# A two-layer transformer kernel: the first norm moved one step ahead, new engine orders in stage one, the rope sum in two pieces

## The reference

```python
xn = layernorm(x)
q, k, v = split(xn @ Wqkv.T + bqkv)            # then rmsnorm of q and k, rope, relu
vk = einsum('bhlp,bhld->bhpd', [v, 1], k)      # linear attention, 16 heads of 8
attn = einsum(vk, q)[..., :-1] / (einsum(vk, q)[..., -1:] + eps)
x = x + rmsnorm(attn @ Wout.T + bout) + quantise6(xn) @ quantise6(W).T + bias
```

## Time and profile before

| | |
|---|---|
| median of 3 runs | 407.57 us (407.36 to 408.72) |
| the profiled execution | 408.92 us, its span 407.1 us |
| busy: PE / DVE / ACT / POOL | 323.2 / 344.1 / 188.4 / 235.4 us |
| last operation of steps 1, 2, 6, 8, 9 | 29.79, 47.08, 109.98, 140.99, 154.96 us |
| routing begins on VectorE | 170.81 us |

### The profile page before, as it was taken

One profiled execution on the slowest core, in us unless ns is written; L12 is line 12 of the kernel. 1 busy time (PEld: TensorE's weight loads), 2 busy tenths in 40 slices (PEclk: granted clock), 3 DMA queues, 4 the chain that ended last, 5 costly groups with the idle time before them and its releaser, 6 DMA issues.

```text
span 407.1 us, 5016 instructions
## 1 busy us (share of the span) xinstructions
PE 323.2 (79%) x1455; PEld 237.0 (58%) x1455; DVE 344.1 (85%) x831; ACT 188.4 (46%) x501; POOL 235.4 (58%) x149
## 2 busy tenths in 40 slices
PE   0267696898898875805129999999999999999995
PEld 0136475777787765704016666666666666666662
DVE  3774997987887964599999899999999999999791
ACT  0535556778678656702122262624426262442521
POOL 9151573553644721095065959778695986867450
PEclk9986998999999999775758999999999999999999
DMA  7620000100100102220000000000000000000000
GB/s 184 209 77 1 2 0 1 54 37 17 52 22 32 53 27 96 91 52 0 1 0 1 2 0 27 2 26 0 0 28 1 26 2 26 1 2 26 0 26 27
DMA packets 13247, 12.49 MB, mean 31 GB/s; under 512 B 1548, under 2 KB 9924, under 8 KB 13220
## 3 DMA queue, kind: packets, MB, share of 16 engines
q1 hardware_dynamic: 10944, 10.10, 7.7%
q0 software_dynamic: 736, 0.95, 1.2%
q10 hardware_dynamic: 1540, 1.12, 0.9%
HBM read 5.88 MB, written 2.10 MB: 20 GB/s over the span
## 4 chain that ended last, share of the span: by engine, by line
PE 54%; DVE 19%; ACT 11%; issue 7%; POOL 6%; DMA 1%; ACTq 1%; POOLq 0%; DVEq 0%
PE Q L833 18%; PE VK L833 16%; PE T L833 9%; PE ND L833 6%; PE T L829 4%; ACT xn L546 4%; POOL prod_qk L773 3%; POOL prod_pv L783 2%; PE Q L829 2%; ACT qkv L503 1%; DMA headmask<-in_c_headsel 1%; ACT Q L585 1%; DVE chosen L1411 1%; DVE bst L1086 1%; DVE scr L1341 1%
## 5 line engine op out<-in xcount | busy, mean ns | idle before, releaser
L783 POOL TENSOR_TENSOR prod_pv<-prob,qkv 128x1024 f32<-128x1024 f32 x32 | 69.6, 2212 | 45.0 <-DVE att L1358 24.3
L686 ACT ACTIVATE sg<-Q 128x512 f32<-128x512 f32 x72 | 43.2, 599 | 97.7 <-PE Q L833 95.0
L773 POOL TENSOR_TENSOR prod_qk<-qkv 128x1024 f32<-128x1024 f32 x32 | 75.9, 2397 | 16.7 <-DVE scr L1341 16.7
L833 PE MATMUL VK<-hid,w 128*128 128x512 f32 x144 | 74.5, 599 | 0.0
L833 PE MATMUL Q<-xT_hi,w_hi 128*128 128x512 f32 x72 | 52.3, 726 | 0.7 <-ACT combT L672 0.7
L1441 DVE TENSOR_TENSOR sgc<-ND,sg 128x512 f32<-128x512 f32 x64 | 43.6, 681 | 6.7 <-PE ND L833 4.7
L1454 DVE TENSOR_TENSOR hid<-T,sgc 128x512 f32<-128x512 f32 x64 | 43.5, 679 | 0.3
L833 PE MATMUL T<-xT_hi,w_hi 128*128 128x512 f32 x72 | 28.9, 401 | 17.0 <-DVE hid L1454 17.0
L833 PE MATMUL Q<-bias,ones 128*128 128x384 f32 (+1 forms) x64 | 32.8, 512 | 9.4 <-ACT qkv L503 5.8
L1341 DVE TENSOR_REDUCE scr<-prod_qk 128x128 f32<-128x1024 f32 x32 | 38.4, 1205 | 0.0
L1358 DVE TENSOR_REDUCE att<-prod_pv 128x128 f32<-128x1024 f32 x32 | 38.2, 1195 | 0.0
(11 more groups left out here) (190 smaller groups left out, 796.9 us busy)
## 6 DMA issues: line engine op xcount, KB each, us to landing
xT_hi<-xTs_hi SPq DMA_DIRECT2D x8, 256.0 KB, 2.3
xT_lo<-xTs_lo SPq DMA_DIRECT2D x8, 256.0 KB, 2.3
out_x<-fin SPq DMA_DIRECT2D x8, 256.0 KB, 2.3
x<-in_x SPq DMA_DIRECT2D x2, 256.0 KB, 4.7
wraw<-in_w1T SPq DMA_DIRECT2D x1, 512.0 KB, 10.8
w<-in_w2T SPq DMA_DIRECT2D x1, 512.0 KB, 4.6
wraw<-in_w3T ACTq DMA_DIRECT2D x1, 512.0 KB, 3.1
sel<-in_c_sel POOLq DMA_DIRECT2D x4, 128.0 KB, 2.8
```

The costliest lines, as they stand in the source:

```text
L686: act.activation(sg[:, side(half, s), :], QB[side(half, s)][:, :], ACT.Silu).then_inc(sg_ready, 1)
L773: pool.tensor_tensor(prod_qk[:, t % 2], bc(qkv2[:, TH * half + t, j, 0:D], 1, NB), qkv2[:, :, j, D:2 * D], ALU.mult).then_inc(qk_prod, 1)
L783: pool.tensor_tensor(prod_pv[:, t % 2].rearrange("p (h e) b -> p b h e", e=HD), bc(prob[:, t], 3, HD), qkv2[:, :, j, 2 * D:QKV].rearrange( ...
L833: return pe.matmul(o, lhsT, rhs, start=start, stop=stop)
```

## The change

xn gets a second buffer. The statistics of the first norm and xn itself are made one step earlier (xn of chunk i in the middle of step i, its statistics in step i - 1), so that step 0, which was empty on ScalarE and VectorE, makes xn of chunk 0 and the statistics of chunk 1. The orders of the parts on ScalarE, TensorE and VectorE in stage one are new. The evacuation of xd's transposes waits for the ffn product that reads the buffer. GpSimd adds the rope products of tiles 0 and 1, and then of tiles 2 and 3. The indices of the norm semaphores move by one, readers of `xn` take `xn[:, c % 2]`, and those of `rope_sum` wait for 2c + 2; ScalarE's last step has its two waits moved by one in the same way. These lines are left out below, with the rest that does not move.

```diff
-        xn = sba("xn", [P, NJ, D])
+        xn = sba("xn", [P, 2, NJ, D])
...
@@ ScalarE @@
             def xn_tiles(c):
-                after(act, mx_y, c)
-                normalise_tiles(xn, x[:, c], 0, range(NJ)).then_inc(xn_ready, 1)
+                after(act, mx_y, c - 1)
+                normalise_tiles(xn[:, c % 2], x[:, c], 0, range(NJ)).then_inc(xn_ready, 1)
             def xdT_evac(c):
-                evac(xdT[:, :, :], tiles(T1), (xdT_ps, c + 1), [], xdT_ready)
+                evac(xdT[:, :, :], tiles(T1), (xdT_ps, c + 1), [(ffn_ps, c)], xdT_ready)
+            def norms_rooted(i):
+                act.wait_ge(ln_value, LNV * (i + 1))
+                act.wait_ge(rms_value, i + 1)
+                act.activation(root[:, 1, :], root[:, 0, :], ACT.Sqrt).then_inc(rooted, 1)
             def step(i):
-                if after_first(i):
-                    act.wait_ge(ln_value, LNV * i)
-                    act.wait_ge(rms_value, i)
-                    act.activation(root[:, 1, :], root[:, 0, :], ACT.Sqrt).then_inc(rooted, 1)
+                norms_rooted(i)
+                weights_of_step(i)
+                run(i, 1, xnT_evac)
+                run(i, 2, xdT_evac)
                 run_next(i, 5, l1_tile(2))
-                weights_of_step(i)
-                if after_first(i):
-                    act.wait_ge(rsqrt_step, RSQ * i)
-                run(i, 1, xn_tiles)
-                run_next(i, 5, l1_tile(3))
-                run(i, 2, xdT_evac)
-                run(i, 1, xnT_evac)
-                run(i, 2, qfT_evac)
+                act.wait_ge(rsqrt_step, RSQ * (i + 1))
                 run(i, 4, xn2_tiles(0))
                 run(i, 4, xn2_tiles(1))
+                run_next(i, 5, l1_tile(3))
+                run(i, 2, qfT_evac)
+                if i == 0:
+                    xn_tiles(0)
                 run(i, 1, qkv_tile(0))
                 run(i, 1, qkv_tile(1))
+                if i > 0:
+                    run(i, 0, xn_tiles)
                 run(i, 4, xn2T_hi_evac)
+                run(i, 1, qkv_tile(2))
                 run(i, 2, attnT_evac)
-                run(i, 1, qkv_tile(2))
...
+                run(i, 1, qkv_tile(3))
                 run(i, 4, l1_tile(0))
-                run(i, 1, qkv_tile(3))
                 run(i, 2, out_squares)
                 run(i, 4, l1_tile(1))
...
@@ GpSimd @@
             def rope_add(c):
-                pool.wait_ge(qkv_rope, NJ * c + NJ)
                 after(pool, feat_ready, c)
                 after(pool, qfT_ps, c)
-                pool.tensor_tensor(rope_ab[:, :, :, :].rearrange("p j n f -> p j (n f)"), rope_a[:, :, :],
-                                   rope_b[:, :, :], ALU.add).then_inc(rope_sum, 1)
+                for h in range(2):
+                    js = slice(2 * h, 2 * h + 2)
+                    pool.wait_ge(qkv_rope, NJ * c + 2 * h + 2)
+                    pool.tensor_tensor(rope_ab[:, js].rearrange("p j n f -> p j (n f)"), rope_a[:, js, :],
+                                       rope_b[:, js, :], ALU.add).then_inc(rope_sum, 1)
...
@@ TensorE @@
             def step(i):
+                run(i, 1, xn_transposes)
+                run(i, 3, ffn_product)
+                run(i, 2, xd_transposes)
                 run_next(i, 5, l1_tile(2))
-                run(i, 3, ffn_product)
+                run(i, 1, qkv_tile(0))
+                run(i, 2, qf_transposes)
                 run_next(i, 5, l1_tile(3))
-                run(i, 2, xd_transposes)
-                run(i, 1, xn_transposes)
-                run(i, 2, qf_transposes)
+                run(i, 1, qkv_tile(1))
                 run(i, 2, value_product)
-                run(i, 1, qkv_tile(0))
-                run(i, 1, qkv_tile(1))
+                run(i, 4, xn2_transposes(i))
                 run(i, 2, numerators)
-                run(i, 4, xn2_transposes(i))
                 run(i, 1, qkv_tile(2))
                 run(i, 1, qkv_tile(3))
                 run(i, 2, attn_transposes(i))
...
@@ VectorE @@
             def ln_values(i):
-                run(i, 0, lambda c: dve.wait_ge(stats1_ready, c + 1))
+                run(i, -1, lambda c: dve.wait_ge(stats1_ready, c + 1))
...
-            ln_values(0)
-            rms_values(0)
+            ln_values(-1)
+            rms_values(-1)
...
             def step(i):
-                if at(i, 0):
-                    return
+                run(i, 1, mx_maxima)
                 rsqrt(i)
-                if at(i, 1):
+                if i == 0:
                     rope_table(1)
                     rope_table(0)
...
+                run(i, 2, features)
                 run(i, 3, projection_scaled)
-                run(i, 2, features)
                 if at(i, 3):
                     vu_scaled(k_l0)
-                run(i, 1, mx_maxima)
                 run(i, 1, mx_scales)
...
                 run(i, 2, attention)
-                run(i, 4, xn2T_lo_part)
                 run(i, 1, rope_tile(2))
                 run(i, 1, rope_tile(3))
-                run(i, 0, stats(0, stats1_ready))
+                run(i, 4, xn2T_lo_part)
+                run(i, -1, stats(0, stats1_ready))
                 run(i, 3, stats(1, stats2_ready))
```

More of the change, by code:

```diff
@@ L600, in l1_tile @@
                 return part
+            def norms_rooted(i):
+                act.wait_ge(ln_value, LNV * (i + 1))
+                act.wait_ge(rms_value, i + 1)
+                act.activation(root[:, 1, :], root[:, 0, :], ACT.Sqrt).then_inc(rooted, 1)
             def step(i):
-                if after_first(i):
-                    act.wait_ge(ln_value, LNV * i)
-                    act.wait_ge(rms_value, i)
-                    act.activation(root[:, 1, :], root[:, 0, :], ACT.Sqrt).then_inc(rooted, 1)
+                norms_rooted(i)
+                weights_of_step(i)
+                run(i, 1, xnT_evac)
+                run(i, 2, xdT_evac)
                 run_next(i, 5, l1_tile(2))
-                weights_of_step(i)
-                if after_first(i):
-                    act.wait_ge(rsqrt_step, RSQ * i)
-                run(i, 1, xn_tiles)
-                run_next(i, 5, l1_tile(3))
-                run(i, 2, xdT_evac)
-                run(i, 1, xnT_evac)
-                run(i, 2, qfT_evac)
+                act.wait_ge(rsqrt_step, RSQ * (i + 1))
                 run(i, 4, xn2_tiles(0))
                 run(i, 4, xn2_tiles(1))
+                run_next(i, 5, l1_tile(3))
+                run(i, 2, qfT_evac)
+                if i == 0:
+                    xn_tiles(0)
                 run(i, 1, qkv_tile(0))
                 run(i, 1, qkv_tile(1))
+                if i > 0:
+                    run(i, 0, xn_tiles)
                 run(i, 4, xn2T_hi_evac)
+                run(i, 1, qkv_tile(2))
                 run(i, 2, attnT_evac)
-                run(i, 1, qkv_tile(2))
-                if isinstance(i, int) and i == STEPS - 2:
+                if i == STEPS - 2:
                     high_part(w3_hi[:, :], wraw[:, :], ld_w3, 32, w3_hi_ready)
                     return
+                run(i, 1, qkv_tile(3))
                 run(i, 4, l1_tile(0))
-                run(i, 1, qkv_tile(3))
                 run(i, 2, out_squares)
@@ L734, in mx_over_scale @@
                 pool.wait_ge(mx_scale, 3 * c + 3)
-                pool.tensor_tensor(blocks(mxy), blocks(xn), bc(amax[:, 2, :], 2, MXB), ALU.mult)\
+                pool.tensor_tensor(blocks(mxy), blocks(xn[:, c % 2]), bc(amax[:, 2, :], 2, MXB), ALU.mult)\
                     .then_inc(mx_y, 1)
@@ L866, in xn_transposes @@
                 after(pe, attnT_ready, c - 1)
-                transposes(T0, lambda j: xn[:, j, :], signal=xnT_ps)
+                transposes(T0, lambda j: xn[:, c % 2, j, :], signal=xnT_ps)
             def qf_transposes(c):
-                pe.wait_ge(rope_sum, c + 1)
+                pe.wait_ge(rope_sum, 2 * c + 2)
                 pe.wait_ge(xdT_ready, c + 1)
@@ L1098, in ln_values @@
                 t.then_inc(ln_value, 1)
-                dve.wait_ge(ln_value, LNV * i + 1)
+                dve.wait_ge(ln_value, LNV * (i + 1) + 1)
                 V.tensor_scalar(root[:, 0, 0:2 * NJ].rearrange("p (n j) -> p n j", j=NJ), mv[:, :, :, 1], LN_EPS,
@@ L1109, in rsqrt @@
             def rsqrt(i):
-                at = RSQ * (i - 1)
-                dve.wait_ge(rooted, i)
+                at = RSQ * i
+                dve.wait_ge(rooted, i + 1)
                 V.reciprocal(root[:, 2, :], root[:, 1, :]).then_inc(rsqrt_step, 1)
@@ L1217, in mx_maxima @@
                 dve.wait_ge(xn_ready, c + 1)
-                V.tensor_reduce(amax[:, 0, :], blocks(xn), AX_X, ALU.max, apply_absolute_value=True)\
+                V.tensor_reduce(amax[:, 0, :], blocks(xn[:, c % 2]), AX_X, ALU.max, apply_absolute_value=True)\
                     .then_inc(mx_scale, 1)
@@ L1253, in features @@
             def features(c):
-                dve.wait_ge(rope_sum, c + 1)
+                dve.wait_ge(rope_sum, 2 * c + 2)
```

## The result

| | before | after |
|---|---|---|
| median, run side by side | 408.65 us (406.96 to 411.96, 20 runs) | 405.67 us (403.51 to 408.82, 20 runs) |
| profiled execution | 408.92 us, span 407.1 | 408.82 us, span 405.9 |

The ratio is 0.9928, its 95% interval 0.9906 to 0.9951: some 3 us faster, where no measurable change was forecast. The two profiled executions hardly differ, though. The runs of either kernel spread over 5 us, and the profiled one of the changed kernel is the slowest of its 20.

A forecast was written before the change was run, and what follows sets the result against it. No engine is full, so a ring of waits sets stage one's 15.5 us step. The terms +1.2, -1.6, +1.15, -0.4 and -0.3 sum to +0.05 us on the 407.57 median: 407.6 us, range 403.8 to 411.

The forecast's parts named there:

- the start: Steps 0 and 1: chunk 1's statistics behind the rope tables delay the first xnT evacuation; +1.15 us by step 1's end.
- the ring: Steady steps of stage one: waits closed across TensorE and VectorE, 16.1 us a step (lower bound 16.0) against 15.5 to 15.6.
- the end of step 1: VectorE's last operation there: 30.0, 31.1 or 32.2 us depending on GpSimd's rope sums; 31.1 taken, against 29.95.
- steps 2 to 4: Stage one after the first steps: 46.0 us, from 16.9 for step 2 and 29.1 for the next two.
- step 9: Value product 1.1 us earlier, numerators losing 0.8 behind the xn2 transposes: -0.3 us on 13.97.
- Steps 3 and 4: No L1 tiles 2 and 3, so a shorter head: 4.9 and 4.8 us to head blocks, about 2.4 shorter together.
- the low clock in step 2: TensorE at 1.2 GHz for much of that step, which takes 16.9 us, -0.4 against 17.29.
- a high clock: TensorE at 2.4 GHz in step 2, which would then take 14.5 us.
- the late evacuation: ScalarE's evacuation of xnT(0) starts near 20.0 us instead of 17.93, 2.05 late, and all of step 1 with it.
- rival 2: Pipeline head: line 1100 ahead of both sum halves (-1.1), high clock in step 2 (-2.4); one 405.5, both 404; chance 0.22.
- Rival 1: Stage one's steps: ring broken somewhere, VectorE or TensorE bounds, 1.5 to 1.9 us gained a step, 398 us; chance 0.06.
- Rival 3: GpSimd holds VectorE in the ring, steps 16.5 us, plus 1.1 in step 1: 411 us; chance 0.33 with milder forms.

The follow-up runs named there:

- warm: Changed kernel with ten idle matmuls on TensorE, six at the end of step 1 and four in step 2; 403.99 us, ratio 0.9887.
- evac_late: Changed kernel with ScalarE's evacuations of xnT, xdT and L1 tile 2 put back behind its wait for rsqrt; 414.23 us, ratio 1.0121.
- norm_only: Norm one step ahead and rope sum in two, but ScalarE, TensorE and VectorE in the orders of the kernel before; 415.01 us, ratio 1.0143.
- xn_at_head: Changed kernel with ScalarE's xn tiles directly behind the wait for rsqrt, ahead of the xn2 tiles; 405.84 us, ratio 0.9921.
- dve_old: Changed kernel with VectorE's head of the step in the old order: rsqrt, projection, features, then the maxima; 406.00 us, ratio 0.9921.
- one_sum: Changed kernel with GpSimd's rope sum in one piece again; 405.31 us, ratio 0.9912.
- magic_late: Changed kernel with VectorE's rounding mx_magic moved behind xn2T_lo; 412.02 us, ratio 1.0078.
- value_first: Changed kernel with TensorE's value product ahead of qkv tile 1, L1 tile 3 after the numerators, and that tile evacuated later; 397.68 us, ratio 0.973.
- stats_first: Changed kernel with VectorE's two rope tables made in step 1 rather than step 0; 405.85 us, ratio 0.9911.
- after_again: Changed kernel run again without edit, for a second profile; 405.34 us, ratio 0.9911, 11 runs.

## Why the prediction was wrong

It forecast a loss at the start and in the ring and a gain in between that cancel. The ring's loss came, somewhat smaller, and so did the gain in between; what failed is the position it gave for the end of step 1, which stands on a hold that the other profiles do not show.

The terms, against the mean of the two profiles of each kernel, forecast in brackets: step 1 +0.6 us (+1.15), steps 2 to 4 -4.0 (-2.8), steps 5 to 8 +1.25 (+1.95), step 9 +0.2 (-0.3), together -1.9 (+0.05). Since the hold falls now before the end of step 1 and now behind it, steps 1 and 2 are better taken as one: -1.3 and -1.0 in the two pairs, where +0.75 was forecast (47.08 to 45.76, 45.20 to 44.16). Steps 3 and 4 gained 2.2, and 2.4 was forecast. The profiles thus give 1.9 us of the 3 us of the medians; the rest they do not show.

*The ring, steps 5 to 8.* Forecast 16.1 (16.0 to 16.3), measured 15.92. The step closes where I said: L1 tile 0 starts behind xn2T_lo after 1.27 us of idling, head blocks wait 2.2 us, and two experiments that open the ring on either side shorten it. The sum of the links was 0.2 a step too high, 0.7 us over four steps; the measured step lies a little under the lower bound of 16.0. The kernel lost 1.25 us here.

*Steps 2 to 4.* Forecast 46.0; measured 46.54 and 44.16, against 48.76 and 49.93 before. The forecast for the low clock in step 2 was 16.9 (measured 16.72), for a high clock 14.5 (13.82 in `warm`); from the step's end to head blocks in steps 3 and 4 I gave 4.9 and 4.8, and 4.69 and 4.79 came (second profile). This is where the kernel gains, 4.0 us in the mean of the two pairs. `evac_late` and `norm_only` show what it needs: that ScalarE no longer holds the evacuation of xn's transposes behind the five small operations and four xn tiles. In step 3 it starts 0.44 us after the step's end (46.20 less 45.76), where it stood 4.05 before (51.13 less 47.08), as these lines of ScalarE's timelines show, first the changed kernel, then the one before:

```profile
46.20 0.59 ACT L503 ACTIVATE xnT<-T 128x512 f32<-128x512 f32 x1
```

```profile
51.13 0.60 ACT L503 ACTIVATE xnT<-T 128x512 f32<-128x512 f32 x1 [0.27 <-PE T L829]
```

Putting 1.4 us of that back in step 3 (2.0 in step 2) costs 2.8 us in step 2 and 1.0 each in steps 3 and 4, against the second profile of the changed kernel; making xn early while keeping the queue behind it costs more than it gives. The runs show no part of the gain in xn's own place on ScalarE (`xn_at_head`), in the order of VectorE's head (`dve_old`) or in the split sum (`one_sum`). TensorE's new order, with xn's transposes first, was not tried alone.

*The start: the step that failed.* "In step 1 this gives an end at 30.0 (line 1100 gets in ahead of both), 31.1 (between) or 32.2. I take 31.1." What came was the first, and 0.8 better still: line 1111 ends at 29.20. The 2.05 us for the late evacuation were right (rope tile 0 at 22.39, 22.6 forecast). But from there to line 1105 it was 6.35 us, not the 7.03 of the profile of before (20.58 to 27.61), and so the line was ahead of the sums. That need not be the work of the change: in the second profiles it is 6.63 us in both kernels. In all four profiles the sum starts 4.21 us after the start of VectorE's last rounding operation; the line starts 4.31 after it in the first profile of before and 3.90 or 3.91 in the other three. What differs is the third qkv tile, whose pair of matmuls took 1.48 us there, 1.03 in the second profile of before and 0.81 in both of after. Why it took longer is open: the granted clock of that stretch, 20 to 26 us, is 1.00 in all four. Of the 2.9 us between the forecast's end of step 9 (155.0) and the mean of the two profiles (152.15), 2.0 lie in this term, 0.7 in the ring, 0.65 in steps 2 to 4, and step 9 gives 0.5 back.

Behind it stands a mistake of method. The 2.27 us of the first profile of before was the base of the term, and it is the exception: in the sixteen other profiles of this case the operation in its place takes at most 0.39 us in step 1, but for 1.22 in `magic_late`, where a rounding operation holds it. And I weighed who gets in ahead of whom and took the middle case, but the case was decided by a margin of 0.3 us (28.74 against 29.05) that I had not worked out. GpSimd starts its sums when rounding and xd are done, and those moved by 1.54 us (27.51 to 29.05), while line 1105 moved by 1.13 (27.61 to 28.74): 0.10 too late became 0.31 early. Against the second profile of before, in which the same line escapes, the start does cost what I had said: 28.86 against 26.84, 2.0 us. It is then the price of filling step 0, and steps 2 to 4 pay it back more than twice. Part of that is the hold itself. In the second profile of before it delays the four xn tiles of step 2 and all behind them; in the changed kernel xn's evacuation no longer waits for the held line 1120 (ScalarE starts it at 30.21 us, the held line ends at 31.60), and TensorE has qkv tiles to do meanwhile. So the hold need cost nothing there. That is read from the profiles; no run tests it, but the equal time of `one_sum` fits.

*Step 9.* Forecast -0.3; measured 0.0 and +0.4.

*The rivals.* In its number, what happened is rival 2 at its first half, 405.5 in a rival of chance 0.22: line 1105 ahead of both halves, and in the first profile no high clock in step 2. The median is 405.67. That the number fits so well is partly luck: against the second profile of before line 1105 gains nothing, and the gain comes from steps 2 to 4. Rival 1's price was about right for a ring that is opened: it gave 398, and `value_first` took 397.68. In the change itself the ring stayed closed. Rival 3, GpSimd holding VectorE in the ring, did not come: line 1237 takes 0.49 us where 0.42 was normal. It comes in `magic_late` at another place, the five small operations: 2 us of holding a step, of which the step grows by 0.34.

*The held operations.* That VectorE's operation waits for the end of GpSimd's is what every case here shows (29.24 and 29.21; 31.60 and 31.55; 97.54 and 97.51). The Trainium skill (SBUF — State Buffer, "SBUF: two separate sides") says an instruction keeps the lock for its whole length, and the trace agrees. By that rule the prediction had the sum 1.1 us higher in step 1; it was not, since neither half held anybody there, the hold having moved to line 1120 in step 2.

*What stays open.* Why the runs of `stats_first` fall more often in its longer group. Where the last 1 us of the medians' 3 comes from. And how far the clock makes the 3 us. At nearly equal means some gain is left: the eight of the changed kernel's 20 runs at 0.940 or 0.941 took 405.5 us on average, the five at 0.941 of the 25 runs of before beside `after_again` 407.9. But an equal mean does not say that the clock was low in the same places.

## What to carry to other kernels

Making something a step ahead gains by what its old consumer's queue may then do at once, not by the operation itself: let the evacuation behind it go ahead too, or, as here, nothing comes of it. Draw the ring of waits across the engines' orders before choosing them, and keep an operation that a whole engine waits for (the value product, the low part) ahead of work that nobody waits for; here that was worth 10 us, three times the change. And where an order is decided by a few tenths of a microsecond, take a second profile before putting a number on it.

## What the runs showed of the hardware

A single hold by GpSimd is short, but it moves: in two profiles of one kernel it fell on an operation of some 0.17 us, which took 2.27, or on one of 0.18 us in the next step, which took 1.58. Splitting the GpSimd operation in two lets VectorE in once between the halves and holds its next operation for the second, 0.51 and 1.18 us, so nothing is won (ratio 0.9997).

Executions of the same kernel differ in TensorE's mean granted clock and by some 4 us, 403.6 us at 0.944 and 407.8 at 0.937 in one set of 11, but in the set of 20 the means do not order the times. From 30 to 35 us the granted clock was 0.51 and 0.66 in two profiles of the changed kernel; with ten idle matmuls just before it was 1.00, and head blocks came at 34.05 us instead of 35.55 in the better of the two.
